# Sampling matmuls in two column groups of 64 pixels, and TensorE's work ordered by pairs of steps

## The chip, the cores and the metric

The kernel runs on one core of a Trainium2 chip. The metric is the device time of one execution in microseconds (us). TensorE's clock has two levels, 1.2 and 2.4 GHz; a granted clock of 1.00 in the profile is 2.4 GHz.

## The reference, cut to what matters

Four layers of the form x = x + f(group_norm(x)) are applied to x of shape (2, 192, 96, 96). The change is in the first one, in its two deformable 3x3 convolutions of 180 channels:

```python
offs = conv1x1(xr, w_offset, b_offset)           # xr: 180 channels, 96 x 96
off_w, off_h = offs[:, :cm], offs[:, cm:]
f_w = deform_conv2d(xr, off_w, w_dcnw, b_dcnw)   # 10 groups of 18 channels, 9 taps
f_h = deform_conv2d(xr, off_h, w_dcnh, b_dcnh)
# in deform_conv2d, for each pixel, group and tap: a bilinear sample of xr at
# (y + ky + dy, x + kx + dx); then
out = jnp.einsum('bikhw,oik->bohw', patches, weight.reshape(Cout, Cin, KK))
```

## The kernel before, in words

The program is a row of phases. The one of interest is `sample_and_convolve` (the tiles named `dc_...` in the profile). It works on tiles of 128 pixels, 72 for each of two images. A tile takes NB = 20 steps: two convolutions (`conv`) of NG = 10 channel groups (`g`) of CG = 18 channels each. The loop body holds NRB = 4 tiles, so NBB = 80 steps, and is written out in full; it runs 36 times in all (2 images, 18 groups of tiles, each in a `Fori` loop whose count `nw` is read from data and is 1 here), which makes 2880 steps, plus 6 ahead of the loop.

One step `n` goes through the engines as follows.

- SyncE loads the horizontal positions of a pair of steps by one broadcasting DMA (`pair_load`, line 742, 864 KB) into one of RP = 8 slots of HX. It waits for `s_free`, which TensorE gives once for each pair.
- ScalarE turns the positions of a pair into hat weights, max(0, 1 - |x - column|), with `distance` (line 778) and `hats` (line 783). Four small activations for the vertical weights (`row_weights`, lines 794 and 797) come in every 20 steps.
- TensorE samples horizontally, `sample(m)`, line 829: for each of 9 taps one matmul whose stationary operand is HX (96 columns of the picture by 128 pixels) and whose moving operand is 6 rows by 18 channels of the picture (XW), 108 elements. The result lies in PSUM, in PT[m % 2], pixels on the partitions. In float32 one matmul is two weight loads and two matmul records in the trace, so a step has 18 of each. TensorE samples LEAD = 6 steps ahead of the step whose convolution it does.
- VectorE multiplies PT by the vertical weights, `weigh(m)`, line 965, into Zt. The six rows are then added up: GpSimd halves them (`halve`, line 896), VectorE does the rest for a pair of steps at a time (`quarter`, line 977, and `sum_rows`, line 985), into VA, pixels on the partitions, 162 values a step.
- TensorE turns VA (line 859) into PR in pieces of 128 values: `pieces` gives each step 1 or 2 of the 13 pieces that 10 steps fill. VectorE copies them from PSUM into VT (`unload`, line 955). TensorE then multiplies them by the convolution's weights WD (line 870), 180 outputs, and adds up in PF. After 10 steps VectorE adds PF to ACC and to a sum (`add_up`); TensorE turns ACC (`turn_sum`, line 838), VectorE copies it (`keep_sum`, line 946) and SyncE stores it.

The order of each engine's queue is written out by hand. TensorE's in one step is: wait for `s_va`; the turns of step n; `sample(n + 6)`, behind a wait for the weights (`s_hx`, line 826); wait for VectorE's copy (`s_vt`, line 865); the convolution of step n. That a PT buffer is free again before it is sampled into follows from `s_va`: GpSimd gives it in `halve`, for an odd step two at a time, after it has waited for `s_z` of the step before. VectorE's order in one step is: `unload(n)`; `rows` in some; `quarter` or `sum_rows`; `weigh(n + 6)`; `add_up` in every tenth.

Of the kernel before, what the change touches and what calls it, by code (L numbers as in the profile page):

```python
# [13 lines left out]
B, C, CM, H, W = 2, 192, 180, 96, 96  # L14
HW = H * W
NG, TAPS, CG = 10, 9, 18
NT = HW // 128
WIN = 6
NWIN = 17
NCK = -(-NG * TAPS * CG // 128)  # L20
# [631 lines left out]
def sample_and_convolve(nc, k):  # L652
# [9 lines left out]
    NB = 2 * NG  # L662
    NRB = 4
# [3 lines left out]
    EXTRA = AHEAD // 2 + 1  # L667
    HALF = WIN // 2 * CG
    LEN = TAPS * CG
    pieces = [range(LEN * g // 128, LEN * (g + 1) // 128) for g in range(NG - 1)]  # L670
    pieces.append(range(LEN * (NG - 1) // 128, NCK))
    with Phase(nc, "dc") as p:
        WD = p.sb([128, NCK, 2, CM])
        XW = p.sb([W, 2, WIN + 2, CM])
# [8 lines left out]
        ZH = p.sb([128, 4, TAPS, HALF])  # L683
        ZQ = p.sb([128, 2, 2 * TAPS, CG])
        VA = p.sb([128, 2, NG * LEN])
        VT = p.sb([128, 2, 2, 128])
        ACC = p.sb([128, NRB, 2, CM])
        FT = p.sb([HM, 2, 4, 128])
        QX = p.sb([W, 1])
# [19 lines left out]
        with p.block() as blk:  # L709
# [109 lines left out]
            @blk.tensor  # L819
            def _(e):  # L820

                def sample(m):
                    i, j, g = m // NB % 2, m % NB, m % NG
                    if j == 0:
                        e.wait_ge(s_xw[i], 16).then_inc(s_xw[i], -16)
                    e.wait_ge(s_hx, 1).then_inc(s_hx, -1)  # L826
                    for t in range(TAPS):
                        ky = t // 3
                        ins = e.matmul(PT[j % 2][:, t // 3, (t % 3) * WIN * CG:(t % 3 + 1) * WIN * CG],  # L829
                                       HX[:, m // 2 % RP, m % 2, t * 128:(t + 1) * 128],  # L830
                                       XW[:, i, ky:ky + WIN, g * CG:(g + 1) * CG],
                                       start=True, stop=True)
                    ins.then_inc(s_t, 1)

                def turn_sum(i, conv):

                    for h in range(2):
                        ins = e.transpose(PR[0:HM, (2 + h) * 128:(3 + h) * 128], ACC[:, i, conv, h * HM:(h + 1) * HM],
                                          k.ident[:, :])
                    return ins  # L840

                for m in range(2):
                    sample(m)
                for m in range(2, LEAD):
                    e.wait_ge(s_pt, 1).then_inc(s_pt, -1)
                    if m % 2:
                        e.sem_inc(s_free, 1)
                    sample(m)
                e.wait_ge(s_pt, 1).then_inc(s_pt, -1)
                e.wait_ge(s_w, 16).then_inc(s_w, -16)  # L850

                def body(b, y2, w):
                    for n in range(NBB):
                        j = n % NB
                        conv, g = j // NG, j % NG
                        e.wait_ge(s_va, 1).then_inc(s_va, -1)
                        for u, c in enumerate(pieces[g]):
                            o = min(128, NG * LEN - 128 * c)
                            ins = e.transpose(PR[0:o, u * 128:(u + 1) * 128],  # L859
                                              VA[:, n // NG % 2, 128 * c:128 * c + o], k.ident[:, :])  # L860
                        if g == 2:
                            ins = turn_sum((n - 12) // NB % NRB, conv ^ 1)
                        ins.then_inc(s_tr, 1)
                        sample((n + LEAD) % NBB)
                        e.wait_ge(s_vt, 1).then_inc(s_vt, -1)
                        if g == 0:
                            e.wait_ge(s_ff, 1).then_inc(s_ff, -1)
                        for u, c in enumerate(pieces[g]):
                            o = min(128, NG * LEN - 128 * c)
                            ins = e.matmul(PF[:, conv * CM:(conv + 1) * CM], VT[0:o, n % 2, u, :],  # L870
                                           WD[0:o, c, conv, :], start=(c == 0), stop=(c == NCK - 1),
                                           skip_group_check=True)
                        if g == NG - 1:
                            ins.then_inc(s_f, 1)
                        elif j % 2 == 0:
                            ins.then_inc(s_free, 1)

                loops(e, body)
                e.wait_ge(s_ff, 1).then_inc(s_ff, -1)
                turn_sum(NRB - 1, 1).then_inc(s_tr, 1)  # L880
                e.wait_ge(s_hx, AHEAD - LEAD).then_inc(s_hx, LEAD - AHEAD)
                e.wait_ge(s_va, 2).then_inc(s_va, -2)

            @blk.gpsimd
            def _(e):
                def halve(n):

                    z = Zt[:, n % 4, :].rearrange("p (t m) -> p t m", t=TAPS)
                    if n >= 2:
                        if n % 2:  # L890
                            e.wait_ge(s_sum, 1).then_inc(s_sum, -1)
                            e.sem_inc(s_va, 2)
                        else:
                            e.wait_ge(s_qt, 1).then_inc(s_qt, -1)
                    e.wait_ge(s_z, 1).then_inc(s_z, -1)  # L895
                    e.tensor_tensor(ZH[:, n % 4, :, :], z[:, :, 0:HALF], z[:, :, HALF:2 * HALF], ALU.add)\  # L896
                        .then_inc(s_half, 1)

                def keep(i):

                    e.wait_ge(s_cr[i % 2], 32).then_inc(s_cr[i % 2], -32)
                    e.tensor_scalar(ACC[:, i, :, :], ACC[:, i, :, :], KF[:, i:i + 1], None, ALU.mult).then_inc(s_pre, 1)
                    e.wait_ge(s_pre, 1).then_inc(s_pre, -1)
                    e.tensor_tensor(ACC[:, i, :, :], ACC[:, i, :, :], CR[:, i, :].rearrange("p (v c) -> p v c", v=2),
                                    ALU.add).then_inc(s_acc, 1)

                def body(b, y2, w):
                    for n in range(NBB):
                        halve(n + 5)
                        if n % NB == 2:  # L910
                            keep(n // NB)

                for n in range(5):
                    halve(n)
                loops(e, body)
                e.wait_ge(s_z, 1).then_inc(s_z, -1)

            @blk.vector
            def _(e):
# [23 lines left out]
                def keep_sum(i, conv):  # L943
                    if conv == 0:
                        e.wait_ge(s_st[i], 16).then_inc(s_st[i], -16)
                    e.tensor_copy(FT[:, i, 2 * conv:2 * conv + 2, :].rearrange("p h x -> p (h x)"), PR[0:HM, 256:512])\
                        .then_inc(s_out, 1)

                def unload(n):
                    e.wait_ge(s_tr, 1).then_inc(s_tr, -1)  # L950
                    if n % NG == 2:
                        keep_sum((n - 12) // NB % 2, n // NG % 2 ^ 1)
                    for u, c in enumerate(pieces[n % NG]):
                        o = min(128, NG * LEN - 128 * c)
                        ins = e.tensor_copy(VT[0:o, n % 2, u, :], PR[0:o, u * 128:(u + 1) * 128])  # L955
                    ins.then_inc(s_vt, 1)

                def weigh(n):
# [27 lines left out]
                                    ZQ[:, n // 2 % 2, :, :], z[:, :, 2 * CG:3 * CG], ALU.add).then_inc(s_sum, 1)  # L986

                def body(b, y2, w):
                    for n in range(NBB):
                        m = n + 5  # L990
                        unload(n)
                        if m % NB in (7, 9, 11, 13):
                            rows((m // NB + 1) % NRB, (m % NB - 7) // 2)
                        if m % 2 == 0:
                            quarter(m - 2)
                        else:
                            sum_rows(m - 3)
                        weigh(m + 1)
                        if n % NG == NG - 1:
                            add_up(b, n // NB, n // NG % 2)  # L1000

                for s in range(4):
                    rows(0, s)
                weigh(0)
                p.tick(e, s_pt)
                weigh(1)
                p.tick(e, s_pt)
                weigh(2)
                p.tick(e, s_pt)
                quarter(0)  # L1010
                weigh(3)
                p.tick(e, s_pt)
                sum_rows(0)
                weigh(4)
                p.tick(e, s_pt)
                quarter(2)
                weigh(5)
                loops(e, body)
                e.wait_ge(s_tr, 1).then_inc(s_tr, -1)
                keep_sum(1, 1)  # L1020
                e.wait_ge(s_half, 1).then_inc(s_half, -1)
                e.wait_ge(s_qt, 1).then_inc(s_qt, -1)
                e.wait_ge(s_hy, 1).then_inc(s_hy, -1)


# [1612 lines left out]
```

## Time and profile before

| | us |
|---|---|
| time, median of 3 runs | 12838.14 (12830.45 to 12851.75) |
| the profiled execution | 12837.92 |
| its span | 12836.0 |
| TensorE matmul busy, whole span | 12028.4 (94%) |
| ScalarE busy | 10370.3 (81%) |
| VectorE busy | 10179.2 (79%) |
| GpSimd busy | 5808.6 (45%) |
| line 829 alone: matmuls, weight loads | 6248.7, 6054.1 |

`sample_and_convolve` runs from about 550 us to about 8002 us of the span. Within it the page's slices are alike from 1000 us on, so any stretch of it stands for the whole. A mean duration of a matmul is longer than the distance between two of them, since they are pipelined; distances are read from where groups of records begin.

### The profile page before, as it was taken

What the parts mean: (1) busy time and instruction counts of PE and PEld (TensorE: products, weight loads), DVE (VectorE), ACT (ScalarE), POOL (GpSimd) and SP (SyncE); (2) the same over time, 40 slices, a digit from 0 to 9 for tenths busy, and PEclk for the clock granted to TensorE, in tenths of its full rate; (3) what the DMA queues carried; (4) which work ended last, traced back from release to release, by engine and by line L of the source; (5) the groups of instructions that cost most, each with busy time, mean ns of one, the idle gap of its engine ahead of it and who ended that gap; (6) DMA issues with size and microseconds to landing.
All of it is one profiled execution on the core that took longest, in us unless ns stands there. A gap on an engine that the chain in (4) does not pass through costs nothing. (4 is left out here: it accounts for less than half of the span.)

```text
span 12836.0 us, 234931 instructions
## 1 busy us (share of the span) xinstructions
PE 12028.4 (94%) x81108; PEld 9861.5 (77%) x81108; DVE 10179.2 (79%) x15927; ACT 10370.3 (81%) x10330; POOL 5808.6 (45%) x3910
## 2 busy tenths in 40 slices
PE   7799999999999999999999999984299899999999
PEld 4599999999999999999999999431253355555555
DVE  5577777777777777777777777689878788888888
ACT  3488888888888888888888887268778799898988
POOL 0144444444444444444444444013310188888887
PEclk9799999999999999999999999597699899999999
DMA  6577777777777777777777777744544433333332
GB/s 180 153 195 193 192 193 193 194 193 193 193 195 193 192 193 194 193 193 192 194 194 192 193 194 181 193 141 152 152 148 161 147 99 106 102 106 100 106 101 84
DMA packets 850569, 2138.18 MB, mean 167 GB/s; under 512 B 108323, under 2 KB 447185, under 8 KB 707169
## 3 DMA queue, kind: packets, MB, share of 16 engines
q1 hardware_dynamic: 833904, 2090.65, 61.3%
q10 hardware_dynamic: 15120, 30.71, 0.7%
q8 instruction: 674, 11.04, 0.4%
q14 instruction: 487, 3.98, 0.1%
q0 software_dynamic: 384, 1.79, 0.0%
HBM read 1827.33 MB, written 295.56 MB: 165 GB/s over the span
## 5 line engine op out<-in xcount | busy, mean ns | idle before, releaser
L829 PE MATMUL dc_p<-dc_t 96*128 96x108 f32 x51948 | 6248.7, 274 | 33.3 <-PEq L826 33.3
L829 PEld LDWEIGHTS dc_p<-dc_t 96*128 96x128 f32 x51948 | 6054.1, 193 | 54.1 <-issue 33.8
L896 POOL TENSOR_TENSOR dc_t<-dc_t 128x486 f32<-128x486 f32 x2885 | 3057.9, 1060 | 4102.6 <-POOLq L895 3796.9
L965 DVE TENSOR_TENSOR dc_t<-dc_p,dc_t 128x972 f32<-128x972 f32 x2886 | 3378.8, 1171 | 1606.6 <-DVEq L963 1598.7
L778 ACT ACTIVATE dc_t<-dc_t 96x2304 f32<-96x2304 f32 x1447 | 3191.9, 2206 | 427.0 <-ACTq L777 426.4
L783 ACT ACTIVATE dc_t<-dc_t 96x2304 f32<-96x2304 f32 x1446 | 3048.3, 2108 | 0.0
L2480 DVE TENSOR_TENSOR_SCAN ms_t<-ms_t,ms_p 128x512 f32<-128x512 f32 x1728 | 2128.4, 1271 | 282.5 <-PE ms_p L2422 203.6
L2396 POOL TENSOR_TENSOR ms_t<-ms_t 128x1536 f32<-128x1536 f32 x576 | 1988.3, 3458 | 503.1 <-DVE ms_t L2480 499.3
L2432 PE MATMUL ms_p<-ms_t,top_t 128*128 128x512 f32 x3456 | 1774.6, 596 | 0.0
L870 PE MATMUL dc_p<-dc_t 128*128 128x180 f32 (+1 forms) x7488 | 1669.6, 323 | 0.0
L2422 PEld LDWEIGHTS ms_p<-top_t,ms_t 128*128 128x128 f32 x6912 | 850.8, 141 | 966.5 <-issue 692.7
L2368 ACT ACTIVATE ms_t<-ms_t 128x384 f32<-128x384 f32 x2304 | 1222.7, 603 | 24.2 <-PE ms_p L2422 24.2
L870 PEld LDWEIGHTS dc_p<-dc_t 128*128 128x128 f32 (+1 forms) x7488 | 1140.4, 191 | 0.1
L2375 ACT ACTIVATE ms_t<-ms_t 128x512 f32<-128x512 f32 x1728 | 1114.5, 709 | 0.0
L2422 PE MATMUL ms_p<-top_t,ms_t 128*128 128x128 f32 x6912 | 1049.2, 275 | 56.4 <-DVE ms_t L2480 50.5
L955 DVE COPY dc_t<-dc_p 128x128 f32<-128x128 f32 (+1 forms) x3744 | 979.1, 281 | 0.5 <-DVEq L950 0.5
L859 PE MATMUL dc_p<-top_t,dc_t 128*128 128x128 f32 (+1 forms) x3744 | 881.0, 273 | 0.0
L794 ACT ACTIVATE dc_t<-dc_t 128x540 f32<-128x540 f32 x290 | 187.2, 645 | 744.7 <-ACTq L792 734.5
L977 DVE TENSOR_TENSOR dc_t<-dc_t 128x324 f32<-128x324 f32 x1442 | 720.3, 500 | 24.9 <-DVEq L975 10.2
L985 DVE TENSOR_TENSOR dc_t<-dc_t 128x324 f32<-128x324 f32 x1441 | 701.4, 487 | 0.0
L2432 PEld LDWEIGHTS ms_p<-ms_t,top_t 128*128 128x128 f32 x3456 | 522.2, 191 | 15.8 <-DVE ms_t L2490 11.5
L859 PEld LDWEIGHTS dc_p<-top_t,dc_t 128*128 128x128 f32 (+1 forms) x3744 | 522.8, 140 | 9.9
(255 smaller groups left out, 9569.8 us busy)
## 6 DMA issues: line engine op xcount, KB each, us to landing
dc_t<-sxd SPq DMA_DIRECT2D x1447, 864.0 KB, 5.8
ms_t<-bcd SPq DMA_DIRECT2D x576, 256.0 KB, 3.3
dc_t<-xrT SPq DMA_DIRECT2D x145, 540.0 KB, 8.1
kvd<-wk_t SPq DMA_DIRECT2D x18, 1536.0 KB, 5.1
szd<-mi_t SPq DMA_DIRECT2D x36, 768.0 KB, 4.3
xvd<-mi_t SPq DMA_DIRECT2D x36, 768.0 KB, 4.7
dld<-mi_t SPq DMA_DIRECT2D x36, 768.0 KB, 3.4
ms_t<-dld SPq DMA_DIRECT2D x36, 768.0 KB, 6.6
```

The lines of the kernel that those rows point to most:

```text
L778: e.activation(HX[:, q % RP, :, :], HX[:, q % RP, :, :], ACT.Abs, bias=QX[:, 0:1]).then_inc(s_ab, 1)
L783: e.activation(HX[:, q % RP, :, :], HX[:, q % RP, :, :], ACT.Relu, bias=1.0, scale=-1.0)\
L829: ins = e.matmul(PT[j % 2][:, t // 3, (t % 3) * WIN * CG:(t % 3 + 1) * WIN * CG], HX[:, m // 2 % RP, m % 2, t * 128:(t + 1) * 128], XW[:, ...
L859: ins = e.transpose(PR[0:o, u * 128:(u + 1) * 128], VA[:, n // NG % 2, 128 * c:128 * c + o], k.ident[:, :])
L870: ins = e.matmul(PF[:, conv * CM:(conv + 1) * CM], VT[0:o, n % 2, u, :], WD[0:o, c, conv, :], start=(c == 0), stop=(c == NCK - 1), skip_gr ...
L896: e.tensor_tensor(ZH[:, n % 4, :, :], z[:, :, 0:HALF], z[:, :, HALF:2 * HALF], ALU.add)\
L965: e.tensor_tensor(Zt[:, n % 4, :].rearrange("p (b m i) -> p b m i", b=3, i=CG), PT[n % 2][:, :, 0:3 * WIN * CG].rearrange("p b (m i) -> p ...
L2368: ins = e.activation(BU[:, i % RT, tb, :], UT[:, c % 2, tb, 0:DI], ACT.Copy, scale=UT[:, c % 2, tb, DI + n:DI + n + 1])
L2396: e.tensor_tensor(G[:, i % RG, :, :], HH[:, i % RH, :, :], CB[:, i % RB, :].unsqueeze(1).to_broadcast([128, ND, T]), ALU.mult).then_inc(s_ ...
L2422: ins = e.transpose(PB[:, d, tb * 128:(tb + 1) * 128], BU[:, i % RT, tb, d * 128:(d + 1) * 128], k.ident[:, :])
L2432: e.matmul(PY[:, d, :], k.ident[:, :], G[:, i % RG, d, :], start=(n == 0), stop=(n == NS - 1))\
L2480: e.tensor_tensor_scan(HH[:, i % RH, d, :], DA[:, i % RA, d, :], PB[:, d, :], CAR[:, n, d:d + 1], ALU.mult, ALU.add).then_inc(s_scan, 1)
```

## The change

Each sampling matmul of 128 pixels becomes two of 64 pixels. The first takes columns 0 to 63 of TensorE's array and writes partitions 0 to 63, the second columns 64 to 127 and partitions 64 to 127. They read the same moving operand. The turns and the convolution stay whole matmuls.

TensorE's loop goes by pairs of steps: the turns of both, `sample(n + 6)` and `sample(n + 7)`, then the convolution of both. `pieces` is cut by pairs, as 2, 3, 2, 3 and 3 of the 13. VectorE's `unload` copies the pieces of a pair in one copy (two for the last pair, whose last piece has 84 rows). The turn of the sum moves from step 2 to step 4 of each ten. `sample` now waits on a semaphore `s_pt` of its own, which GpSimd gives at the head of `halve` as soon as `weigh` is through. `s_free` is given once for each pair, behind the first piece of the convolution. VectorE's order in a pair is `unload`, `rows`, `weigh(n + 6)`, `quarter(n + 4)`, `weigh(n + 7)`, `sum_rows(n + 4)`, `add_up`.

```diff
-    pieces = [range(LEN * g // 128, LEN * (g + 1) // 128) for g in range(NG - 1)]
-    pieces.append(range(LEN * (NG - 1) // 128, NCK))
+    NPR = NG // 2
+    pieces = [range(2 * LEN * g // 128, 2 * LEN * (g + 1) // 128) for g in range(NPR - 1)]
+    pieces.append(range(2 * LEN * (NPR - 1) // 128, NCK))
...
-        VT = p.sb([128, 2, 2, 128])
+        VT = p.sb([128, 2, 3, 128])
...
                     for t in range(TAPS):
                         ky = t // 3
-                        ins = e.matmul(PT[j % 2][:, t // 3, (t % 3) * WIN * CG:(t % 3 + 1) * WIN * CG],
-                                       HX[:, m // 2 % RP, m % 2, t * 128:(t + 1) * 128],
-                                       XW[:, i, ky:ky + WIN, g * CG:(g + 1) * CG],
-                                       start=True, stop=True)
+                        for o in (0, 64):
+                            ins = e.matmul(PT[j % 2][o:o + 64, t // 3, (t % 3) * WIN * CG:(t % 3 + 1) * WIN * CG],
+                                           HX[:, m // 2 % RP, m % 2, t * 128 + o:t * 128 + o + 64],
+                                           XW[:, i, ky:ky + WIN, g * CG:(g + 1) * CG],
+                                           start=True, stop=True, tile_position=(0, o))
...
                 def body(b, y2, w):
-                    for n in range(NBB):
-                        j = n % NB
-                        conv, g = j // NG, j % NG
-                        e.wait_ge(s_va, 1).then_inc(s_va, -1)
+                    for n in range(0, NBB, 2):
+                        conv, g = n // NG % 2, n % NG // 2
+                        e.wait_ge(s_va, 2).then_inc(s_va, -2)
...
                         if g == 2:
-                            ins = turn_sum((n - 12) // NB % NRB, conv ^ 1)
+                            ins = turn_sum((n - 14) // NB % NRB, conv ^ 1)
                         ins.then_inc(s_tr, 1)
-                        sample((n + LEAD) % NBB)
+                        for m in (n + LEAD, n + LEAD + 1):
+                            e.wait_ge(s_pt, 1).then_inc(s_pt, -1)
+                            sample(m % NBB)
                         e.wait_ge(s_vt, 1).then_inc(s_vt, -1)
...
-                            ins = e.matmul(PF[:, conv * CM:(conv + 1) * CM], VT[0:o, n % 2, u, :],
+                            ins = e.matmul(PF[:, conv * CM:(conv + 1) * CM], VT[0:o, n // 2 % 2, u, :],
                                            WD[0:o, c, conv, :], start=(c == 0), stop=(c == NCK - 1),
                                            skip_group_check=True)
-                        if g == NG - 1:
+                            if u == 0:
+                                ins.then_inc(s_free, 1)
+                        if g == NPR - 1:
                             ins.then_inc(s_f, 1)
-                        elif j % 2 == 0:
-                            ins.then_inc(s_free, 1)
...
                 def halve(n):
+                    e.wait_ge(s_z, 1).then_inc(s_z, -1)
+                    e.sem_inc(s_pt, 1)
                     if n >= 2:
                         if n % 2:
                             e.wait_ge(s_sum, 1).then_inc(s_sum, -1)
                             e.sem_inc(s_va, 2)
                         else:
                             e.wait_ge(s_qt, 1).then_inc(s_qt, -1)
-                    e.wait_ge(s_z, 1).then_inc(s_z, -1)
...
                 def unload(n):
                     e.wait_ge(s_tr, 1).then_inc(s_tr, -1)
...
-                    for u, c in enumerate(pieces[n % NG]):
-                        o = min(128, NG * LEN - 128 * c)
-                        ins = e.tensor_copy(VT[0:o, n % 2, u, :], PR[0:o, u * 128:(u + 1) * 128])
+                    full = sum(128 * (c + 1) <= NG * LEN for c in pieces[g])
+                    ins = e.tensor_copy(VT[:, n // 2 % 2, 0:full, :].rearrange("p u x -> p (u x)"), PR[:, 0:full * 128])
+                    if full < len(pieces[g]):
+                        o = NG * LEN % 128
+                        ins = e.tensor_copy(VT[0:o, n // 2 % 2, full, :], PR[0:o, full * 128:(full + 1) * 128])
                     ins.then_inc(s_vt, 1)
...
                 def body(b, y2, w):
-                    for n in range(NBB):
-                        m = n + 5
+                    for n in range(0, NBB, 2):
                         unload(n)
-                        if m % NB in (7, 9, 11, 13):
-                            rows((m // NB + 1) % NRB, (m % NB - 7) // 2)
-                        if m % 2 == 0:
-                            quarter(m - 2)
-                        else:
-                            sum_rows(m - 3)
-                        weigh(m + 1)
-                        if n % NG == NG - 1:
+                        if n % NB in (2, 4, 6, 8):
+                            rows((n // NB + 1) % NRB, n % NB // 2 - 1)
+                        weigh(n + 6)
+                        quarter(n + 4)
+                        weigh(n + 7)
+                        sum_rows(n + 4)
+                        if n % NG == NG - 2:
                             add_up(b, n // NB, n // NG % 2)
```

## Rows read from the trace of the kernel before

**Rows 1.** The page's part 2, TensorE's rows: forty slices of the span.
```profile
PE   7799999999999999999999999984299899999999
PEld 4599999999999999999999999431253355555555
...
PEclk9799999999999999999999999597699899999999
```
**Rows 2.** Busy time by window; the window's length stands first.
```profile
core 0: us, PE busy (x) PEld busy (x) DVE busy (x) ACT busy (x) POOL busy (x), PEclk, DMA share, GB/s
1000.00:8000.00 7000.00, 7000.00 (x60118) 6968.58 (x60118) 5505.14 (x10472) 5970.71 (x3263) 3164.72 (x2993) 1.00 0.76 193
```
**Rows 3.** Groups of instructions, 4000 to 6000 us: count, busy, mean ns, idle before.
```profile
L829 PE MATMUL dc_p<-dc_t 96*128 96x108 f32 x13995 | 1676.6, 273 | 0.0
L829 PEld LDWEIGHTS dc_p<-dc_t 96*128 96x128 f32 x13995 | 1624.0, 192 | 5.4
L965 DVE TENSOR_TENSOR dc_t<-dc_p,dc_t 128x972 f32<-128x972 f32 x777 | 909.7, 1171 | 421.3 <-DVEq L963 419.5
...
L955 DVE COPY dc_t<-dc_p 128x128 f32<-128x128 f32 (+1 forms) x1011 | 264.4, 281 | 0.0
...
L859 PEld LDWEIGHTS dc_p<-top_t,dc_t 128*128 128x128 f32 (+1 forms) x1010 | 140.7, 139 | 2.6
...
L946 DVE COPY dc_t<-dc_p 90x256 f32<-90x256 f32 x77 | 31.6, 410 | 0.0
```
**Rows 4.** TensorE's timeline, two steps: start, length, line, count of records.
```profile
4001.59 2.16 PE L829 MATMUL dc_p<-dc_t 96*128 96x108 f32 x18
4003.59 0.49 PE L870 MATMUL dc_p<-dc_t 128*128 128x180 f32 x2
4003.91 0.27 PE L859 MATMUL dc_p<-top_t,dc_t 128*128 128x128 f32 x1
4004.02 2.16 PE L829 MATMUL dc_p<-dc_t 96*128 96x108 f32 x18
```
**Rows 5.** VectorE's timeline in the same steps.
```profile
4002.56 0.28 DVE L955 COPY dc_t<-dc_p 128x128 f32<-128x128 f32 x1
4002.99 0.50 DVE L977 TENSOR_TENSOR dc_t<-dc_t 128x324 f32<-128x324 f32 x1
4003.90 1.17 DVE L965 TENSOR_TENSOR dc_t<-dc_p,dc_t 128x972 f32<-128x972 f32 x1 [0.41 <-DVEq L963]
```
**Rows 6.** Matmuls of the fourth layer's phase, timeline, TensorE.
```profile
9572.56 1.45 PE L2103 MATMUL mi_p<-mi_t 96*128 96x512 f32 x3
9573.94 1.91 PE L2111 MATMUL mi_p<-mi_t 128*44 128x512 f32 x4
9575.78 1.12 PE L2103 MATMUL mi_p<-mi_t 96*128 96x512 f32 x2
```
**Rows 7.** The same stretch, weight loads.
```profile
9573.93 0.16 PEld L2111 LDWEIGHTS mi_p<-mi_t 128*44 128x44 f32 x2 [0.76 <-issue]
...
9575.78 0.30 PEld L2103 LDWEIGHTS mi_p<-mi_t 96*128 96x128 f32 x2 [0.83 <-issue]
```
**Rows 8.** Timeline of tiny matmuls in the expanding phase, both of TensorE's rows.
```profile
8013.30 0.26 PEld L1121 LDWEIGHTS mx_p<-mx_t 90*1 90x1 f32 x8 [2.36 <-DMA mx_t<-c_ones]
8013.33 0.34 PE L1121 MATMUL mx_p<-mx_t 90*1 90x2 f32 x8 [2.30 <-DVE mx_t L1152]
```
**Rows 9.** The page's part 3, the queue of TensorE's instructions: packets, MB, share.
```profile
q8 instruction: 674, 11.04, 0.4%
```

More of the change, by code:

```diff
@@ L848, in _ @@
                     sample(m)
-                e.wait_ge(s_pt, 1).then_inc(s_pt, -1)
                 e.wait_ge(s_w, 16).then_inc(s_w, -16)
                 def body(b, y2, w):
-                    for n in range(NBB):
-                        j = n % NB
-                        conv, g = j // NG, j % NG
-                        e.wait_ge(s_va, 1).then_inc(s_va, -1)
+                    for n in range(0, NBB, 2):
+                        conv, g = n // NG % 2, n % NG // 2
+                        e.wait_ge(s_va, 2).then_inc(s_va, -2)
                         for u, c in enumerate(pieces[g]):
@@ L882, in _ @@
                 e.wait_ge(s_va, 2).then_inc(s_va, -2)
+                e.wait_ge(s_pt, 1).then_inc(s_pt, -1)
             @blk.gpsimd
@@ L950, in unload @@
                     e.wait_ge(s_tr, 1).then_inc(s_tr, -1)
-                    if n % NG == 2:
-                        keep_sum((n - 12) // NB % 2, n // NG % 2 ^ 1)
-                    for u, c in enumerate(pieces[n % NG]):
-                        o = min(128, NG * LEN - 128 * c)
-                        ins = e.tensor_copy(VT[0:o, n % 2, u, :], PR[0:o, u * 128:(u + 1) * 128])
+                    g = n % NG // 2
+                    if g == 2:
+                        keep_sum((n - 14) // NB % 2, n // NG % 2 ^ 1)
+                    full = sum(128 * (c + 1) <= NG * LEN for c in pieces[g])
[3 more added lines that the diff above has]
+                        ins = e.tensor_copy(VT[0:o, n // 2 % 2, full, :], PR[0:o, full * 128:(full + 1) * 128])
                     ins.then_inc(s_vt, 1)
@@ L1004, in _ @@
                 weigh(0)
-                p.tick(e, s_pt)
                 weigh(1)
-                p.tick(e, s_pt)
                 weigh(2)
-                p.tick(e, s_pt)
                 quarter(0)
                 weigh(3)
-                p.tick(e, s_pt)
                 sum_rows(0)
                 weigh(4)
-                p.tick(e, s_pt)
                 quarter(2)
                 weigh(5)
+                sum_rows(2)
                 loops(e, body)
@@ L1021, in _ @@
                 e.wait_ge(s_half, 1).then_inc(s_half, -1)
-                e.wait_ge(s_qt, 1).then_inc(s_qt, -1)
+                e.wait_ge(s_sum, 1).then_inc(s_sum, -1)
                 e.wait_ge(s_hy, 1).then_inc(s_hy, -1)
```

## The prediction

> **What bounds the kernel now.** I read the page's slices first [rows 1]: from slice 4 to slice 24 TensorE's matmuls and its weight loads both stand at 9 or more, at the full clock. That is the sampling phase, more than half of the time, and the only one that the change touches. The window from 1000 to 8000 us [rows 2] says the same in numbers: matmuls busy 7000 of 7000 us, weight loads 6969, ScalarE 5971, VectorE 5505, GpSimd 3165, the DMA engines 0.76, the clock 1.00. Then the groups of 2000 us [rows 3]: 777 `weigh` (line 965), so a step takes 2000 / 777 = 2.574 us and a pair 5.15 us. TensorE's lines have no idle time before them, VectorE waits 421 us ahead of line 965. So TensorE paces the phase, and every us that a pair of steps loses or gains there counts 1440 times (2880 steps) in the span. Per pair the others need: ScalarE 5.15 x 0.853 = 4.39 us, VectorE 5.15 x 0.786 = 4.05, the DMA engines 5.15 x 0.76 = 3.91.
>
> What TensorE's 5.15 us are made of stands in its timeline [rows 4]. Sampling begins at 4001.59 and the convolution at 4003.59: 18 records in 2.00 us, 0.111 each. The two convolution records take until 3.91 (0.16 each), the turn until 4.02 (0.11). For a pair, with 13 pieces in 10 steps: sampling 36 x 0.111 = 4.00; convolution 2.6 x 0.32 = 0.83; turns, with the sum's, (13 + 2) / 5 = 3.0 x 0.11 = 0.33. The sum is 5.16, against 5.15.
>
> Why 0.111? Two rates compete. A record that streams 180 elements takes (0.32 - 0.01) / 2, about 0.155, and the records with 512 elements follow each other by 0.43 ((1.45 - 0.59) / 2 in [rows 6], where 0.59 is one record's own length, (1.02 - 0.43)); that is 0.84 ns an element (two passes at 2.4 GHz are 0.833), so 108 elements need 0.09 and 2 ns, 0.0925. The load of 128 columns, where it lies open behind a stop, costs 0.10 to 0.11 [rows 6, 7]. Sampling goes at the load's pace, not the stream's: 17% of its time is weight loading that the matmul doesn't cover.
>
> **The change part by part.** *Sampling.* A step's 18 loads of 128 columns become 36 of 64, and its 18 records become 36 of 108 elements. I count in slots of one record for each half of the array; a pair of steps has 36. Call the time of a slot x. What x is the trace doesn't show: no instruction there uses the right half of the array alone, nor two parts at once. Bounds: the stream alone, with both halves at the same time, gives 0.0925; both streams in turn give 0.185. I take 0.0945, the stream and once more the 2 ns between records. The nearest row for the loads is line 2111, with 44 columns [rows 7]: two loads in 0.16 us, each 0.12 long, so 0.04 apart, which scales to 0.055 for 64 columns. A half's load is then hidden under its own stream, if the halves load side by side. Sampling: 36 x 0.0945 = 3.40, from 4.00.
>
> *Switches.* The trace has a place where an array of 44 columns comes between full ones [rows 6]. Line 2103 starts three records from 9572.56, 0.43 apart, so the next would start at 9573.85; line 2111 starts at 9573.94, 0.09 late. Its four records take 1.91 - 0.59 = 1.32 for three distances, 0.03 more than 3 x 0.43: the second load lies open. The next line is due at 9575.69 and comes at 9575.78, 0.09 late again, and its second record comes 0.53 later in place of 0.43. I take this as what a switch between a full and a narrow array costs: 0.09 + 0.05 (a load of 64) going in, 0.09 + 0.10 (of 128) coming out, 0.33 a pair. The order by pairs makes it two switches for two steps, not four. Ends: 0.10, if the loads are pulled ahead, and 0.69, if a switch waits for a matmul's whole length (0.27 less 0.09, twice) and then for the load's (0.14 in, 0.19 out [rows 3]).
>
> *Convolution and turns.* The same records in another order, 0.83 + 0.33 = 1.16.
>
> The sum: 3.40 + 0.33 + 1.16 = 4.89 us a pair, 0.26 less than 5.15. Times 1440 that is 370 us.
>
> The Trainium skill, TensorEngine Tiling (Array Packing), section Key Properties, says that a change of the tiling mode drains TensorE and that tiles load and multiply in parallel. The 0.09 of [rows 6] is what the first half of it looks like here; the second no row shows.
>
> *VectorE.* 13 copies of 0.26 (264.4 / 1011) in ten steps, 3.4 us, become five, and a sixth for the 84 rows. A copy of 256 elements takes 0.41, one of 128 takes 0.28 [rows 3], so one of 384 about 0.54: 3 x 0.41 + 2 x 0.54 + 0.28 = 2.6. VectorE gains 0.16 a pair, worth nothing while it has (5.15 - 4.05) us to spare. *ScalarE* has the same work, 4.39 a pair: it is the next bound, 0.50 below the new 4.89. The DMA share would rise to 0.76 x 5.15 / 4.89 = 0.80.
>
> *Waits.* `sample` now waits for `s_pt`. Behind that wait on TensorE stand both samplings, the convolution and the next turns. It is given when `weigh` two steps earlier is through and GpSimd has come to that `halve`. From the end of `sample(n + 5)` on PE has 0.83 + 0.33 + 0.33 = 1.5 us ahead of `sample(n + 6)`, which wants `weigh(n + 4)`, done before; and 1.7 more until `sample(n + 7)`, which wants `weigh(n + 5)`, 1.17 long [rows 5] from that same end. GpSimd's halving lasts 1.06 and comes once a step, with 45% busy. Nothing, with 1.5 us of cover. The wait for `s_vt` gets safer: the copy that followed the turns by 2.56 + 0.28 - 1.59 = 1.25 us [rows 4, 5] now has both samplings, 3.4 us, to hide in, even with `weigh`, `sum_rows`, `add_up` and `rows` ahead of it (some 3 us). `s_free` comes a step later in the pair; ScalarE's slots hold 8 pairs, some 39 us. The sum's turn moves by two steps, with a store that is not waited for.
>
> *Issue.* A slot has four instructions, one each 24 ns. Eight loads and eight tiny matmuls stand (0.34 - 0.16) / 7 = 0.025 apart as pairs [rows 8], 13 ns an instruction. That is a short run; the stream's 11.04 MB of instructions [rows 9] would grow by some 6 MB, at 0.4% of the DMA engines. I cost both at nothing.
>
> **The rivals.** *B, the loads take turns.* The halves multiply side by side, but the loads share one path. Then a slot is two loads of 64: 0.111 if half a load costs half, 0.117 if each pays the 4 to 6 ns by which 0.111 exceeds 128 columns' own 0.107. The pair is 36 x 0.114 + 1.49 = 5.59, which is 0.44 x 1440 = 640 us slower: 13480 (13340 to 13650). It decides from x = 0.102 on, where 36x + 1.49 is 5.15. For it speaks that the loads are what bounds sampling now, and that the number of columns loaded stays the same; against it, nothing but that the two halves are separate. This is the mechanism that ends on the other side.
>
> *C, the matmuls take turns*, so that splitting only doubles them, and the change doesn't do what it says: x = 0.185, the pair 8.15, 3.0 x 1440 = 4320 us slower, 17160. For it: every pair of records in this trace starts a full stream apart. Against it: none of them lie in different columns.
>
> The Trainium skill, TensorE: Matmul & The Clock Gate, section Part 3, has a rule that speaks against this change: a weight load overlaps matmuls in flight only when the row groups differ, and the two halves here have the same rows. Taken strictly it would have today's records 0.107 + 0.0925 = 0.20 apart; the trace has 0.111, so for a full array it does not hold. For halves it would lead to C or beyond, and lends C some of its chance.
>
> *D, side by side, but dear switches.* x = 0.0945 and the switch's upper end, 0.69: 3.40 + 0.69 + 1.16 = 5.25, which is 0.10 x 1440 = 140 us slower, 12980. Against it are the two places of 0.09.
>
> *E, the gain is larger.* x = 0.0925 and switches of 0.10: the pair is 4.59, 800 us faster, 12030. ScalarE's 4.39 would end it at 1090 us. This is the forecast's own lower end.
>
> **How the numbers follow.** The profiled execution's 12837.92 and the median of 12838.14 are one number. The forecast is 12838 - 370 = 12468 us. Chances: the forecast with its range of 12030 to 12830, 0.60; B 0.19; C 0.12; D 0.07; something else 0.02. The range for 8 in 10 has to take in the forecast, D and B: 12030 to 13650. C is left out. About 0.2% (26 us) is what a measurement of this kernel tells from no change. The forecast's upper edge and D's lower one put 0.05 there: faster 0.57, same 0.05, slower 0.38.
>
> **What would show it.** In the changed kernel's timeline: line 829's records of one step, 36 of them, within 1.7 us (B: 2.0 to 2.1; C: 3.3); the two records of a slot starting within a few ns; from the last turn to the first sampling 0.20, from the last sampling to the first convolution 0.18 and 0.10 more before the second; loads of line 829 overlapping in twos. The pair of steps (twice the distance of line 965's count) 4.9 us, matmuls still without idle time, ScalarE at 0.90 of the window, VectorE at 0.80. Wrong would be: idle time ahead of line 829 put down to `s_pt` or `s_hx`, ScalarE over 0.97, or stops inside line 829 that come from the instruction queue.

## The result and the profile after

The changed kernel takes 12411.68 us (median of 4 runs, 12408.59 to 12423.67) against 12843.21 for the kernel before in the same job: 0.9666 of it, 95% interval 0.9655 to 0.9677, some 430 us less. The profiled execution's span is 12421.6 us.

The window that answers to [rows 2], in the same columns:

```profile
core 0: us, PE busy (x) PEld busy (x) DVE busy (x) ACT busy (x) POOL busy (x), PEclk, DMA share, GB/s
1000.00:7300.00 6300.00, 6253.41 (x103778) 5817.60 (x103777) 5365.91 (x8152) 5674.10 (x3104) 3144.45 (x2848) 1.00 0.82 205
```

TensorE has idle time now, 47 us of 6300. ScalarE stands at 0.90, VectorE at 0.85 (0.80 was forecast), the DMA engines at 0.82. The groups from 4000 to 6000 us, as in [rows 3]:

```profile
L831 PE MATMUL dc_p<-dc_t 96*64 96x108 f32 x29651 | 1471.8, 257 | 12.2 <-issue 9.9 <-PEq L827 2.0
L831 PEld LDWEIGHTS dc_p<-dc_t 96*64 96x64 f32 x29648 | 1381.6, 136 | 88.1 <-issue 87.5
L972 DVE TENSOR_TENSOR dc_t<-dc_p,dc_t 128x972 f32<-128x972 f32 x824 | 961.5, 1167 | 270.7 <-DVEq L970 242.7
```

824 `weigh` in 2000 us make 4.854 us a pair of steps, where 777 made 5.15. Over 1000 to 7300 us it is 4.870. TensorE's timeline, as in [rows 4]:

```profile
4003.27 0.38 PE L859 MATMUL dc_p<-top_t,dc_t 128*128 128x128 f32 x2
4003.59 3.55 PE L831 MATMUL dc_p<-dc_t 96*64 96x108 f32 x72
4007.07 0.88 PE L872 MATMUL dc_p<-dc_t 128*128 128x180 f32 x4
4007.79 0.49 PE L859 MATMUL dc_p<-top_t,dc_t 128*128 128x128 f32 x3
4008.21 3.00 PE L831 MATMUL dc_p<-dc_t 96*64 96x108 f32 x60
```

The 72 sampling records of a pair, twice as many as before, take 3.48 us from the first to the convolution's start, where 36 took 4.00. The two records of a slot start 0.007 us apart, and every second record 0.092 to 0.093 after the one before it: the two halves of the array stream side by side, at the stream's own pace. The two turns start at 4003.27 and 4003.38, the sampling at 4003.59, 0.21 later. The convolution's four records take 0.72, where four at 0.153 take 0.61: its second load lies open, that is, no matmul in flight hides it. With the three terms of the prediction the sum is 36 x 0.0925 = 3.33, switches 0.34 (0.09 and 0.05 going in, 0.09 and 0.10 coming out), convolution and turns 1.13: 4.80. The measured pair is 0.07 longer (4.870). Where that is, the timeline shows in places like this one, the longest of them, with the window behind the stop:

```profile
3790.89 0.49 PE L859 MATMUL dc_p<-top_t,dc_t 128*128 128x128 f32 x3
3791.31 1.79 PE L831 MATMUL dc_p<-dc_t 96*64 96x108 f32 x33
3795.73 3.58 PE L831 MATMUL dc_p<-dc_t 96*64 96x108 f32 x36 [2.63 <-issue]
...
3795.70:3799.30 3.60, 3.57 (x39) 3.53 (x38) 1.57 (x2) 3.47 (x2) 1.04 (x1) 0.50 0.24 58
```

Sampling breaks off after 33 records with no semaphore to wait for ("issue"). Behind the stop, 36 records take 3.58 us, some 0.19 a slot and not 0.0925: the granted clock is 0.50, the lower level. So such a stop costs twice. Laid against the distances of a kernel that has no stops (`split_load`, below, pair 4.801), the window holds some 66 us of stops, 0.05 us a pair, and some 21 us that the lower level costs, 0.016 a pair. It was granted in ten stretches, 44 us in all, and each begins at the end of a stop of 1.8 to 2.9 us or just behind it; three other stops of 1.9 to 2.4 us had none behind them. The kernel before has 0.3 us of stops in such a window and no such stretch. In the DMA records, a 16 KB transfer of TensorE's instruction queue starts at 3792.86 (the one before at 3781.50), takes 1.40 us, and TensorE goes on 1.5 us after its end. There are 37 stops over 0.6 us in sampling between 1000 and 7300 us; their median distance from the end of such a transfer is 1.47 us. Between two transfers TensorE's rows have 256 records on average, its waits counted in (215,798 records, 843 transfers in the window). The queue itself, to be laid beside [rows 9]:

```profile
q8 instruction: 1080, 17.69, 0.6%
```

### The profile page after: what moved, and what is told of

The parts are those of the page before. It is cut to its first block and busy times, and to the rows that moved or that the text cites. A ratio compares the mean times of both kernels' runs of the same rounds, so it can differ in the third digit from the quotient of the medians.

```text
span 12421.6 us, 338253 instructions
## 1 busy us (share of the span) xinstructions
PE 11555.8 (93%) x133056; PEld 8928.9 (72%) x133056; DVE 10330.4 (83%) x13907; ACT 10361.2 (83%) x10330; POOL 5958.3 (48%) x3910
## 5 line engine op out<-in xcount | busy, mean ns | idle before, releaser
L831 PE MATMUL dc_p<-dc_t 96*64 96x108 f32 x103896 | 5162.5, 257 | 85.9 <-issue 44.9
L831 PEld LDWEIGHTS dc_p<-dc_t 96*64 96x64 f32 x103896 | 4847.6, 136 | 353.6 <-issue 351.7
L900 POOL TENSOR_TENSOR dc_t<-dc_t 128x486 f32<-128x486 f32 x2885 | 3169.6, 1099 | 3525.6 <-DVEq L990 2344.8
L872 PE MATMUL dc_p<-dc_t 128*128 128x180 f32 (+1 forms) x7488 | 1537.0, 337 | 0.6 <-PEq L867 0.3
L992 DVE TENSOR_TENSOR dc_t<-dc_t 128x324 f32<-128x324 f32 x1442 | 823.1, 571 | 0.0
L984 DVE TENSOR_TENSOR dc_t<-dc_t 128x324 f32<-128x324 f32 x1442 | 702.0, 487 | 0.2 <-DVEq L982 0.2
L959 DVE COPY dc_t<-dc_p 128x256 f32<-128x256 f32 (+1 forms) x1440 | 673.4, 468 | 9.1 <-DVEq L954 8.7
L859 PE MATMUL dc_p<-top_t,dc_t 128*128 128x128 f32 (+1 forms) x3744 | 646.3, 273 | 0.2 <-PEq L856 0.2
L934 DVE TENSOR_TENSOR dc_t<-dc_t 128x270 f32<-128x270 f32 x580 | 557.8, 962 | 71.6 <-DVEq L932 69.7
```

What stands on the lines that cost most here:

```text
L831: ins = e.matmul(PT[j % 2][o:o + 64, t // 3, (t % 3) * WIN * CG:(t % 3 + 1) * WIN * CG], HX[:, m // 2 % RP, m % 2, t * 128 + o:t * 128 + o ...
L872: ins = e.matmul(PF[:, conv * CM:(conv + 1) * CM], VT[0:o, n // 2 % 2, u, :], WD[0:o, c, conv, :], start=(c == 0), stop=(c == NCK - 1), sk ...
```

## The experiments

**The order without the column groups.** The sampling matmuls are whole again in the changed kernel.

```diff
-                        for o in (0, 64):
-                            ins = e.matmul(PT[j % 2][o:o + 64, ...], HX[..., t * 128 + o:t * 128 + o + 64], XW[...],
-                                           start=True, stop=True, tile_position=(0, o))
+                        ins = e.matmul(PT[j % 2][:, ...], HX[..., t * 128:(t + 1) * 128], XW[...],
+                                       start=True, stop=True)
```

> The changed kernel with the sampling matmuls whole again (128 columns, one matmul a tap): the order by pairs, the merged copies and the new waits alone. Theory (the gain is the column groups', by a slot that falls from 0.111 to the stream's 0.0925 us, less two switches of 0.17 a pair): TensorE's sum for a pair is 36 x 0.111 + 0.83 + 0.33 = 5.16 us as in the kernel before, so 12840 us, within 0.3% of it. Rival (the order and the lighter VectorE bring a part of the 430 us): 12600 to 12750 us. It would be slower than before, 12900 or more, if the new waits cost something when TensorE is the bound.

Measured: 12832.55 us, 0.9992 of before (0.9983 to 1.0002), the pair 5.145 us. Its timeline has 36 records in 4.00 us:

```profile
4003.74 4.17 PE L830 MATMUL dc_p<-dc_t 96*128 96x108 f32 x36
4007.74 1.10 PE L871 MATMUL dc_p<-dc_t 128*128 128x180 f32 x6
```

The order, the new waits and VectorE's merged copies are worth nothing alone, and cost nothing. The merged copies do take less, 0.52 us a pair in place of 0.68, as forecast. But VectorE as a whole gains nothing by it: it is busy for 4.12 us a pair, where it was 4.05. Line 933's mean is 1.01 us, and 0.57 for the same work before (line 930); why is not shown.

**The column groups without the order.** The same two-matmul loop, put into the kernel before.

> The kernel before with the column groups alone, in its order by single steps, so four switches between full and narrow matmuls for a pair of steps, not two. Theory: 36 x 0.0925 + 2 x 0.34 + 0.83 + 0.33 = 5.17 us a pair, against 5.15 before and 4.85 after: 12870 us, no gain left, and the step from the last turn to the first sampling record and from the last one to the convolution still 0.20 and 0.19 us. Rival (a switch costs less than 0.34, and the changed kernel's pair is longer than 4.80 for another reason): 12500 to 12700 us.

Measured: 12838.01 us, 0.9997 of before (0.9988 to 1.0007), the pair 5.148 us. One step of it:

```profile
4001.04 0.27 PE L860 MATMUL dc_p<-top_t,dc_t 128*128 128x128 f32 x1
4001.24 1.89 PE L830 MATMUL dc_p<-dc_t 96*64 96x108 f32 x36
4003.06 0.57 PE L871 MATMUL dc_p<-dc_t 128*128 128x180 f32 x2
4003.47 0.38 PE L860 MATMUL dc_p<-top_t,dc_t 128*128 128x128 f32 x2
```

Sampling a step takes 1.82 us with its switch at the end, not 2.00; then 0.20 from turn to sampling in place of 0.11, and 0.41 for two convolution records in place of 0.32. 0.18 gained, 0.18 lost. Neither half of the change moves the time; only together do they, since the order halves the switches. This kernel has no stops at all, with almost the same number of instructions a step but 5.15 us for a pair: an instruction transfer each 7.9 us, at a DMA share of 0.77.

**Both halves in one column group.** `PT[j % 2][0:64, ...]` and `tile_position=(0, 0)` for both.

> The changed kernel with both halves in the left column group, writing the same 64 partitions (the pixels of the right half are left out). If what shortens a slot is that the halves use different columns, it now takes two whole streams, 2 x 0.0925 = 0.185 us; the pair is 36 x 0.185 + 1.47 = 8.13 us and the time 17100 us. If a narrow matmul were cheaper in itself, a slot would stay near 0.0925 to 0.11 and the time below 13100 us.

Measured: 17108.0 us (one run), the pair 8.123 us, a slot 0.185:

```profile
4000.75 6.87 PE L832 MATMUL dc_p<-dc_t 96*64 96x108 f32 x72
4007.56 0.88 PE L874 MATMUL dc_p<-dc_t 128*128 128x180 f32 x4
```

This is rival C's size to 0.3%. The gain is that the halves lie in different columns, nothing else about narrow matmuls.

**What the whole matmul waits for.** Whole matmuls that stream fewer rows: 54 elements, then 90, the loads unchanged.

```diff
-                                       XW[:, i, ky:ky + WIN, g * CG:(g + 1) * CG],
+                                       XW[:, i, ky:ky + WIN // 2, g * CG:(g + 1) * CG],
```

> The changed kernel with whole sampling matmuls (128 columns) that stream 54 elements in place of 108 (three of six rows are left out). If sampling with whole matmuls goes at the weight load's pace, half the stream saves nothing: records stay 0.111 us apart, the pair 5.15, 12840 us. If the stream had a part in it, records come closer, down to 0.048, and the time falls to 12300 or less.

Measured: 18668.17 us, 1.454 of before (1.4508 to 1.4571). That was not expected by either. The window from 1000 to 7300 us:

```profile
1000.00:7300.00 6300.00, 6300.00 (x30270) 6246.23 (x30270) 2761.30 (x4313) 3036.78 (x1642) 1599.96 (x1506) 0.54 0.43 108
```

And a step of its timeline:

```profile
4000.11 7.77 PE L831 MATMUL dc_p<-dc_t 96*128 96x54 f32 x36
4007.66 1.53 PE L873 MATMUL dc_p<-dc_t 128*128 128x180 f32 x4
```

The granted clock is 0.54 through the phase, so mostly the lower level, 1.2 GHz, with TensorE's row busy for all 6300 us and not one gap. Records are 0.21 apart (36 in 7.55 us), twice the 0.10 to 0.11 of an open load, where a stream of 54 elements at half the clock needs 0.09. So the load's pace shows here too, but at the wrong level for a comparison of times.

> The changed kernel with whole sampling matmuls (128 columns) that stream five of the six rows, 90 elements (the sixth row's samples are left out). With 54 elements the granted clock was 0.54 through the phase, and the time 18668 us, so that run showed the load's pace at 1.2 GHz alone (0.21 us a record). Here the stream is 0.077 us against 0.0925 with six rows. Theory (whole sampling goes at the load's pace): if the clock is granted in full, records stay 0.111 apart, the pair 5.15 us, 12830 us. Rival (the stream has a part in the 0.111): 0.094 to 0.105 a record, 12000 to 12500 us. A clock below 1.00 would lie outside both, and the records' distance then has to be read from stretches at full clock.

Measured: 12834.75 us, 0.9983 of before (0.9972 to 0.9995), clock 1.00, 36 records in 3.99 us:

```profile
4002.42 4.15 PE L831 MATMUL dc_p<-dc_t 96*128 96x90 f32 x36
4006.41 1.11 PE L873 MATMUL dc_p<-dc_t 128*128 128x180 f32 x6
```

A sixth of the stream taken away saves nothing: whole sampling goes at the pace of its weight loads.

**Whether the halves' loads run side by side.** The changed kernel, streaming 54 elements.

> The changed kernel with sampling matmuls that stream 3 of the 6 rows, 54 elements in place of 108 (the other three rows' samples are left out and stay zero). The loads are the same. If the two groups' weight loads run side by side, a slot is the larger of a load of 64 columns, 0.053 to 0.058 us, and the stream, 0.048: about 0.056. If they take turns and were hidden only just by the stream, it is 0.107 to 0.117. The sum for a pair is then 3.5 us in the first case, so that ScalarE's 4.39 us sets the pair, 11750 us; and 5.3 us in the second, 13000 us. Stops for instructions should become frequent in the first case, since four instructions come every 56 ns in sampling.

Measured: 12208.75 us (one run). Of the two cases for a slot the first holds: 18 slots of a step span 1.26 us, less the last record's 0.23, so 0.06 each (0.058 in the median), with two loads of 64 columns in each:

```profile
4000.13 1.26 PE L832 MATMUL dc_p<-dc_t 96*64 96x54 f32 x36 [0.37 <-PEq L828]
...
4005.12 0.82 PE L832 MATMUL dc_p<-dc_t 96*64 96x54 f32 x21 [1.10 <-PEq L828]
4008.20 3.03 PE L832 MATMUL dc_p<-dc_t 96*64 96x54 f32 x51 [2.26 <-issue]
```

In turns they would need 0.107 to 0.117, as was expected. The time missed both figures: the pair is 4.72 us, not ScalarE's 4.39, because sampling now stops again and again, for instructions ("issue", 374 us of 2000 on the load row) and for what stands behind line 828, ScalarE's weights. And the clock is 0.91: 1087 of the 6300 us went at the lower level, in which a slot takes 0.107. The last line shown, behind a stop of 2.26 us, lies in such a stretch (51 records in 3.03 us).

**Four column groups.** `for o in (0, 32, 64, 96)`, 32 pixels each.

> The changed kernel with four sampling matmuls of 32 pixels in four column groups. The streams are the same, the loads half as long, so the array's own time doesn't change: a slot of 0.0925 us and 4.80 us a pair. But a slot has sixteen instructions for each tap in place of eight, one each 12 ns. If the instruction queue keeps up (short runs go at 12.5 ns an instruction), about 12410 us or slightly more; if instructions are what stops TensorE already, at one each 27 ns on the average, the time goes by their number: some 165 instructions a step against 83; at the 16 KB pages' closest distance so far, 4.1 us for 256, that is 2.6 us a step, 5.3 a pair, 13100 us, with stops everywhere in sampling.

Measured: 14651.58 us (one run), 6.41 us a pair:

```profile
4000.92 0.39 PE L831 MATMUL dc_p<-dc_t 96*32 96x108 f32 x6 [2.91 <-issue]
...
4002.37 3.59 PE L831 MATMUL dc_p<-dc_t 96*32 96x108 f32 x144
```

When its instructions are there, TensorE takes 144 records and as many loads in 3.59 us, 12 ns an instruction; issue is not the limit. Supply is: TensorE stands still in gaps of over 0.4 us for some 1100 of 6300 us, 1.1 us a pair, and goes on 1.42 us in the median after the end of an instruction transfer. The lower clock level behind such stops, 949 of 6300 us, costs nearly 0.5 more (an estimate: half of that time, over 983 pairs). With the 4.80 of the records that makes about the 6.41. The direction was expected; the size was put at 5.3 us a pair by the closest distance of two transfers, 4.1 us (the changed kernel's window has one of 3.6). Here they start 5.1 us apart in the median, and the clock was not thought of.

**Half of the position load.** The stops come after late instruction transfers. Are those late because of the other traffic?

```diff
-                    e.dma_start(HX[:, slot, :, :].rearrange("p u n -> p (u n)"), src).then_inc(s_bx[slot], 16)
+                    e.dma_start(HX[:, slot, 0:1, :], src[:, :, 0:NPX]).then_inc(s_bx[slot], 16)
```

> The changed kernel whose load of horizontal positions brings the first step of each pair alone (432 KB in place of 864; the second step's positions are left out, ScalarE and TensorE do the same work on what lies there). The changed kernel's pair takes 4.86 us, 0.06 more than its records' distances give (36 x 0.0925 + 0.34 + 0.80 + 0.33 = 4.80), and the trace shows TensorE's stops of 0.6 to 2.9 us to end 1.2 to 1.7 us after a 16 KB page of TensorE's instructions has landed. Theory (the page is late because its transfer starts behind the position loads on the same DMA engines): with half of that traffic the stops go, 0.058 x 1440 = 83 us less than the changed kernel, 12330 us. Rival (the page is asked for late by TensorE's own sequencer, whatever the DMA engines do): stops as before, 12410 us.

Measured: 12321.76 us, 0.9595 of before (0.9577 to 0.9614), 90 less than the changed kernel. The pair is 4.800 us, the sum of the records' distances, and the stops sum to 0.4 us:

```profile
1000.00:7300.00 6300.00, 6299.84 (x105257) 5873.78 (x105253) 5482.86 (x8270) 5723.70 (x3150) 3199.70 (x2889) 1.00 0.40 116
```

**The same bytes, in two loads.** The load of a pair is issued as one for each step, the first released in the middle of the pair's first sampling, the second by the convolution; `s_free` and `s_bx` count twice.

```diff
+                    for u in range(2):
+                        e.wait_ge(s_free, 1).then_inc(s_free, -1)
+                        e.dma_start(HX[:, slot, u:u + 1, :], src[:, :, u * NPX:(u + 1) * NPX]).then_inc(s_bx[slot], 16)
...
+                        if free and t == 2:
+                            ins.then_inc(s_free, 1)
...
+                            sample(m % NBB, m == n + LEAD)
```

> The changed kernel with the load of a pair's horizontal positions issued as two of 432 KB, one for each step, the first released in the middle of the pair's first sampling and the second by the convolution, some 2.9 us later; bytes and work are those of the changed kernel. Theory (a page of TensorE's instructions is late because it waits behind a burst of position packets; half of the load took all stops away): bursts half as long, a late page by half as late, most stops gone, 40 to 80 us less than the changed kernel, 12330 to 12370 us. Rival (it is the mean load of the DMA engines, 0.82, that counts, not the burst): 12410 us, stops as before.

Measured: 12332.2 us, 0.9597 of before (0.9584 to 0.961). The stops are 1.8 us in 6300, the pair 4.801, and TensorE's time is whole again while as many GB/s move as before:

```profile
1000.00:7300.00 6300.00, 6299.07 (x105225) 5872.53 (x105225) 5479.45 (x8266) 5722.91 (x3149) 3193.86 (x2887) 1.00 0.75 208
```

So it isn't the bytes moved but how and when they come. The split also releases half of a slot some 3 us earlier, and the DMA share falls from 0.82 to 0.75; which of these keeps the instruction transfers in time wasn't told apart. Nor does any run show whether a late transfer was asked for late or stood behind others.

**The convolution in column groups as well**, first on the changed kernel, then with split loads.

```diff
+                            for h in (0, 64):
+                                ins = e.matmul(PF[h:h + 64, conv * CM:(conv + 1) * CM], VT[0:o, n // 2 % 2, u, h:h + 64],
+                                               WD[0:o, c, conv, :], start=(c == 0), stop=(c == NCK - 1),
+                                               skip_group_check=True, tile_position=(0, h))
```

> The changed kernel with the convolution's matmuls also cut in two halves of 64 pixels in the two column groups, so that the switch back to a full array comes ahead of the turns, whose weight load is half as long. Theory: leaving the groups costs 0.10 for the drain and 0.05 for the open load of a turn, in place of 0.10 and 0.10: 0.05 less a pair, 70 us less than the changed kernel, 12340 us. Against it: five more matmuls and loads a pair, which the instruction queue has to bring; if stops for instructions grow with their number, 0 to 20 us of it are lost. Rival (the drain depends on what the next mode's first instruction is, or transposes after narrow matmuls wait longer): 12410 us or more.

Measured: 12451.79 us, 0.9697 of before (0.9681 to 0.9713), 40 us more than the changed kernel. The stops had grown to some 130 us in 6300, and the stretches at the lower clock behind them to 58 us; together they cost 0.12 a pair, where the changed kernel lost 0.07. That ate the gain, which without stops is 0.04.

> The same with the convolution's matmuls in the two column groups too. Without stops the convolution in halves had a pair of 4.881 - 0.105 = 4.78 us against 4.870 - 0.058 = 4.81 for the changed kernel, and lost it by twice the stops. If split loads take the stops away, it is 0.03 to 0.05 us a pair faster than split loads alone, 40 to 70 us: 12280 to 12320 us. If they don't, it is the slower of the two, 12430 or more.

Measured: 12279.77 us, 0.9557 of before (0.9544 to 0.957), the fastest kernel here that does the whole work. The pair is 4.770 us with 17 us of stops:

```profile
4003.74 3.55 PE L832 MATMUL dc_p<-dc_t 96*64 96x108 f32 x72
4007.12 1.09 PE L876 MATMUL dc_p<-dc_t 128*64 128x180 f32 x12
4008.14 0.44 PE L862 MATMUL dc_p<-top_t,dc_t 128*128 128x128 f32 x2
```

From sampling to the convolution there is no switch now (3.38 us in place of 3.48, and no open load behind it); it comes ahead of the turns. The same edit is worth +40 us or -50 us, by whether TensorE's instructions arrive in time.

**What comes next.** Column groups and split loads, streaming five of six rows.

> The kernel with column groups and split loads, with five of the six rows streamed (the sixth row's samples are left out). It asks what comes next once a slot is shorter: at 0.077 us a slot TensorE's sum is 36 x 0.077 + 1.47 = 4.24 us a pair, below ScalarE's 4.39. Theory (ScalarE sets the pair): 4.40 to 4.45 us, 12343 - 0.38 x 1440 = 11800 us, ScalarE busy for 0.98 or more. Rival (TensorE's instructions come too slowly for it, one each 25 ns with the clock as it is): stops in sampling again, 4.5 to 4.75 us, 11900 to 12250 us.

Measured: 11935.13 us, 0.9286 of before (0.9252 to 0.9321), the pair 4.523 us:

```profile
1000.00:7000.00 6000.00, 5743.92 (x106350) 5312.24 (x106349) 5708.12 (x8356) 5795.89 (x3183) 3284.50 (x2917) 1.00 0.80 221
```

Of its waits (who for whom, us in total, times, longest), TensorE's:

```profile
PE dc_p L833 <- PEq L829: 223.7, 338, 1.3
```

The pair and the time lie in the rival's range, but its mechanism is the smaller part: TensorE waits 28 us for instructions ("issue") and 224 us at line 829, for ScalarE's weights. Nor is it the theory's case: ScalarE is at 0.97, not 0.98 or more, with VectorE at 0.95, and the pair is 0.13 above the 4.39 that ScalarE needs. With three engines this close to full none of them runs free; which one costs the 0.13 is open.

## Why the prediction was right

It said 12468 us; the changed kernel took 12412, 56 us less.

- *What bounds.* TensorE, at the pace of its weight loads: shown by `five_rows_whole`, where a shorter stream changes nothing, and by the slot of two loads side by side.
- *The slot*, which no row of the trace before could show, was taken at 0.0945 and is 0.0925: the second half's start, 7 ns behind the first, is hidden in the next slot. That term was 0.07 a pair too high, 100 us.
- *The switches*, read from another phase's matmuls of 44 columns [rows 6], were put at 0.33 a pair and are 0.34. This is the term that decides the sign of the single edit, and `groups_old_order`, with two more of them, stands where it says: no gain.
- *Convolution and turns*: 1.16 against 1.13.
- *Waits, `s_pt`, the copies*: nothing, and `order_only` shows nothing. VectorE was to need 0.16 a pair less, 3.89 us; it needs 4.15, since other lines take longer than the copies save. With the bound elsewhere that cost nothing.
- *Issue and the instruction queue* were costed at nothing, and that was wrong. Issue itself is nothing (12 ns an instruction in the four-group run). But supply costs 0.07 a pair, 99 us, three quarters of it in stops and a quarter by the lower clock behind them, which the prediction didn't think of. It looked at the queue's share of the DMA engines [rows 9], 0.4%, and not at how soon one transfer must come: with twice the instructions in less time one is due each 7.5 us, not 13.9. That alone isn't it, though: at one each 7.9 us and a DMA share of 0.77 (`groups_old_order`), and at one each 7.4 with split loads, there are next to no stops.

The last point and the slot's term have about the same size and opposite signs, so the sum was nearer than its parts, and that is luck. Of the remaining 56 us, 30 are the difference of the pair (4.89 forecast, 4.87 measured). The rest isn't in the sum at all. The phase as a whole takes 7025 us (548.4 to 7573.5) against 7453, 428 less, of which the shorter pair explains 0.277 x 1440 = 399. Some 28 us come from the phase's start, here first in the kernel before, then in the changed one:

```profile
540.00:600.00 60.00, 50.42 (x232) 50.08 (x232) 19.40 (x35) 43.91 (x24) 13.63 (x13) 0.50 0.77 180
540.00:600.00 60.00, 46.31 (x704) 42.85 (x706) 34.38 (x48) 54.34 (x30) 21.25 (x19) 0.83 0.94 215
```

Both enter the phase at the lower clock level. The kernel before stays there for its first 63 us; the changed one has the full clock after 5 us and falls back once, for 7 us. The other traces divide in the same way: with whole sampling matmuls the clock rises 33 to 63 us after the first of them, with narrow ones 4 to 12 us after it. Why is not shown.

The rivals: B, the loads in turns, is refuted by the slot of 0.06 in `half_stream`. C is what one column group does, 17108 against 17160 forecast, and not what two do. D and E were wrong about the switches, the first from above and the second from below; E had the slot right. The rule that was set against the change, that a weight load overlaps matmuls in flight only when the row groups differ (the Trainium skill, TensorE: Matmul & The Clock Gate, Part 3), doesn't hold for these two halves, which have the same rows: with a load behind each stream of 0.0925 the slot could not be 0.0925. That tiles load and multiply in parallel (the Trainium skill, TensorEngine Tiling (Array Packing), Key Properties) the runs do show, and a change of mode costs what a drain would: 0.09 us here, and behind it one load that nothing hides.

## What to carry to other kernels

Where weight loads, not streams, pace a run of matmuls, compare the distance of two records with the stream's time per element; cutting the columns in two groups wins the difference, and each switch to and from full matmuls costs 0.09 us and an open load, so count switches first: here either edit alone was worth nothing. When an edit doubles an engine's instructions, price the arrival of the instructions too, one 16 KB transfer for 256 of them, against the kernel's own transfers, and the lower clock that can follow a stop; splitting the largest load gave 80 us. An edit that is slower by itself may be held back by that alone, so it is worth another try after.

## What the runs showed that was not expected

- TensorE stayed mostly at 1.2 GHz (granted clock 0.54) in an unbroken sequence of whole matmuls of 54 elements behind loads of 128 columns, where the same sequence with 90 elements had 1.00. Both show a row of matmuls that is always busy. A shorter stream behind the same load made the kernel 45% slower; why the clock isn't granted is open.
- Instruction transfers of 1.2 us, hidden altogether at one in 13.9 us, stopped TensorE for up to 2.9 us at one in 7.5 us, with position loads of 864 KB between them, and hardly at all with loads of 432 KB (1.8 us of stops in 6300).
- Ten of the 37 stops over 0.6 us were followed by a stretch at 1.2 GHz, which added a third to what the stops cost.
- Four column groups stream side by side like two: 144 records in 3.59 us against 72 in 3.55.
